# Mixture-of-experts tile loop: transposed rows two tiles ahead, first half's routing moved ahead

## The reference, cut to what matters

```
h      = layernorm(x); h = (h - mean over tokens) / sd over tokens
h      = h * gamma(subject) + beta(subject)              # a small network per batch
probs  = softmax(h @ router_w)                            # 8 experts
gates, idx = top_k(probs, 2); gates = gates / gates.sum(-1)
hid    = relu(h @ exp_w1[e] + exp_b1[e])                  # 128 -> 512, for each expert
eout   = hid @ exp_w2[e] + exp_b2[e]                      # 512 -> 128
out    = x + sum over the two chosen experts of gate * eout
```

## Time and profile before

| | us |
|---|---|
| median of 3 runs | 141.12 |
| lowest and highest | 140.81, 142.25 |
| the profiled execution | 139.6 |
| its span, first to last instruction | 137.8 |
| TensorE busy | 98.7 (72%) |
| DVE busy | 54.7 (40%) |
| ACT busy | 48.7 (35%) |
| GpSimd busy | 47.3 (34%) |

### The profile page before, as it was taken

How to read it: one execution, slowest core, us unless ns; L and a number is a source line. 1 busy time by engine, 2 the same in 40 slices (tenths; PEclk the granted TensorE clock), 3 DMA queues, 4 the chain that set the end, 5 groups by cost and what they waited for, 6 DMA issues and landing times.

```text
span 137.8 us, 2307 instructions
## 1 busy us (share of the span) xinstructions
PE 98.7 (72%) x668; PEld 82.5 (60%) x668; DVE 54.7 (40%) x250; ACT 48.7 (35%) x145; POOL 47.3 (34%) x62
## 2 busy tenths in 40 slices
PE   6999997699999999007866777667777677773000
PEld 2597984498595949006856777567776567763000
DVE  0679988195699160300133222232222332222053
ACT  3615654713806161000543334433344333341000
POOL 7594400006876772000022343223432223434100
PEclk9999999959999999855699999999999999999755
DMA  4999994000110117992041748898988788000183
GB/s 97 351 305 412 412 402 198 2 0 13 44 41 26 40 36 179 415 379 67 0 139 65 233 177 252 270 277 243 237 229 259 230 288 320 8 3 0 52 276 129
DMA packets 12140, 24.47 MB, mean 178 GB/s; under 512 B 1895, under 2 KB 7223, under 8 KB 12128
## 3 DMA queue, kind: packets, MB, share of 16 engines
q1 hardware_dynamic: 9936, 22.01, 48.7%
q0 software_dynamic: 1184, 1.46, 3.2%
q10 hardware_dynamic: 1008, 0.86, 2.1%
HBM read 18.04 MB, written 7.28 MB: 184 GB/s over the span
## 4 chain that ended last, share of the span: by engine, by line
PE 36%; DMA 26%; issue 18%; POOL 8%; DVE 6%; ACT 2%; POOLq 1%; SPq 1%; DVEq 0%; ACTq 0%
PE zt L864 12%; DMA sums_dram<-yg_t,rt 9%; PE zt L874 8%; POOL rows_dram L502 7%; DMA wt<-in_exp_w_dram 7%; DMA rows_dram<-h_row,row_i 4%; DMA rt<-rows_dram 3%; PE zt L686 3%; DMA sums<-sums_dram 2%; PE zt L701 2%; PE zt L828 2%; DVE acc L1244 1%; PE yt L855 1%; PE zt L835 1%; PE aux L746 1%
## 5 line engine op out<-in xcount | busy, mean ns | idle before, releaser
L670 ACT ACTIVATE hid_t<-zt,wt 128x128 f32<-128x128 f32 x84 | 23.9, 368 | 48.5 <-PE zt L864 48.5
L511 POOL DMA_INDIRECT sums_dram<-yg_t,rt x21 | 20.4, 970 | 54.9 <-DVE yg_t L1231 54.6
L864 PE MATMUL zt<-xT_t,wt 128*128 128x128 f32 x168 | 25.6, 299 | 15.9 <-issue 13.4
L864 PEld LDWEIGHTS zt<-xT_t,wt 128*128 128x128 f32 x168 | 22.0, 204 | 19.6 <-issue 15.8
L1231 DVE SCALAR_TENSOR_TENSOR yg_t<-zt,rt,b_t 128x128 f32<-128x128 f32 x21 | 7.4, 351 | 44.6 <-PE zt L874 44.6
L874 PE MATMUL zt<-wt,hid_t 128*128 128x128 f32 x168 | 22.1, 275 | 0.0
L874 PEld LDWEIGHTS zt<-wt,hid_t 128*128 128x128 f32 x168 | 20.5, 193 | 0.0
L502 POOL DMA_INDIRECT rows_dram<-h_row,row_i x16 | 15.8, 988 | 6.0 <-issue 4.3
L621 ACT ACTIVATE hid<-zt,we 128x512 f32<-128x512 f32 x16 | 11.0, 688 | 12.6 <-PE zt L828 11.7
L828 PE MATMUL zt<-h,we 128*128 128x512 f32 x30 | 14.3, 601 | 0.0
L844 PEld LDWEIGHTS yt<-we,hid 128*128 128x128 f32 x64 | 9.0, 227 | 0.5 <-issue 0.5
(11 more groups left out here) (170 smaller groups left out, 116.5 us busy)
## 6 DMA issues: line engine op xcount, KB each, us to landing
wt<-in_exp_w_dram SPq DMA_DIRECT2D x21, 578.0 KB, 5.1
rows_dram<-spare_rows SPq DMA_DIRECT2D x1, 3120.0 KB, 13.1
rt<-rows_dram SPq DMA_DIRECT2D x21, 65.0 KB, 3.5
we<-in_exp_w_dram SPq DMA_DIRECT2D x2, 578.0 KB, 10.3
sums_dram<-zeros SPq DMA_DIRECT2D x2, 512.0 KB, 14.8
f<-in_x_dram SPq DMA_DIRECT2D x2, 256.0 KB, 4.5
ft<-in_x_exchanged_dram SPq DMA_DIRECT2D x2, 256.0 KB, 5.2
sums<-sums_dram SPq DMA_DIRECT2D x4, 128.0 KB, 3.0
```

The source lines that it names most:

```text
L511: pool.indirect_dma_start(sums_dram, bass.IndirectOffsetOnAxis(ap=rt[:, n, ID_AT:ID_AT + 1].bitcast(I32), axis=0), yg_t[:, n, :], None, bo ...
L670: act.activation(hid_t[:, i % 2, c, :], z_t[i % 2][:, c * P:(c + 1) * P], ACT.Relu, bias=bias).then_inc(tile_hid, 1)
L864: last = pe.matmul(z_t[i % 2][:, c * P:(c + 1) * P], wt[:, i % W_SLOTS, c * P:(c + 1) * P], xT_t[:, i % 2, :], start=True, stop=True)
```

## The change

- *Tile loop.* DVE copies the transposed rows of tile i+2, not of tile i+1, before it gates tile i.
- *SP.* The weights of each of the first five tiles are issued as soon as its code is loaded, not after all 21 codes. Twelve codes are loaded before the wait for the row scatters, the others one by one in the alternating loop, behind the row load.
- *Shares.* They are written by DVE into `h_row` directly; GpSimd's copy L495 and its semaphore go.
- *First half's routing.* On TensorE, logits, row transposes and ranks of half 0 move ahead of most of expert 0's layer 1 (which is no longer cut in pairs). On DVE, the choices of half 0 move ahead of the second half's normalising; the shares of half 0 are woven into the second half's inverse deviation (`shares_and_inverse_sd`), and row numbers come before the normalised copies. On ACT the exponential and the row copies of half 0 move ahead.
- *Dense experts.* The order becomes half by half: `turn(e, n)` = 2n + e. Expert 0 and expert 1 on half 0 are computed before expert 0 and 1 on half 1; DVE's gates and additions for half 0 are placed among the second half's front.

The core of the diff (the renamed uses of `share` and of `y_d[e][n]` left out):

```diff
+def turn(e, n):
+    return n * DENSE + e
...
-            codes = [sp.value_load(code[i:i + 1, 0:1], min_val=0, max_val=SPARE) for i in range(TILES)]
+            def next_code():
+                i = len(codes)
+                codes.append(sp.value_load(code[i:i + 1, 0:1], min_val=0, max_val=SPARE))
...
+            sp.wait_ge(code_ready, 1)
             for i in range(W_SLOTS):
+                next_code()
                 tile_weights(i)
+            while len(codes) < CODES_FIRST:
+                next_code()
             sp.wait_ge(rows_out, 16 * B * TOPK)
...
                     tile_rows(i + ROW_SLOTS - W_SLOTS)
+                if len(codes) < TILES:
+                    next_code()
...
-                pool.wait_ge(share_ready, 2 * (n + 1))
-                pool.tensor_copy(h_row[:, :, batches(n), GATE_AT],
-                                 share[:, batches(n), :].rearrange("p b k -> p k b")).then_inc(row_gate_ready, 1)
-                pool.wait_ge(row_gate_ready, n + 1)
+                pool.wait_ge(share_ready, TOPK * (n + 1))
...
-            act.wait_ge(w_in[0], 16)
+            inverse_sd_features(1)
+            gate_exponent(0)
+            token_rows(0)
             hidden(0, 0, 0)
-            inverse_sd_features(1)
-            token_rows(0)
             hidden(0, 0, 1)
             normalise(1)
...
-            layer1_by_pairs()
+            wait_for_h(0)
             logits(0)
+            token_rows(0)
+            layer1(0, 0, 0)
             layer1(0, 0, 1)
+            ranks(0)
             layer1(0, 0, 2)
-            token_rows(0)
+            layer1(0, 0, 3)
+            pe.wait_ge(h_row_ready, TOPK)
+            layer2(0, 0, 0)
             pe.wait_ge(xs_ready, BH)
             norm_transposed(1)
-            layer1(0, 0, 3)
-            ranks(0)
-            pe.wait_ge(h_row_ready, TOPK)
-            layer2(0, 0, 0)
             for c in range(1, C):
                 layer2(0, 0, c)
+            pe.wait_ge(w_in[1], 16)
+            layer1(1, 0, 0)
             wait_for_h(1)
             logits(1)
-            layer1(0, 1, 0)
             token_rows(1)
-            layer1(0, 1, 1)
+            layer1(1, 0, 1)
             ranks(1)
-            layer1(0, 1, 2)
-            layer1(0, 1, 3)
+            layer1(1, 0, 2)
+            layer1(1, 0, 3)
+            pe.wait_ge(acc_done, BH * (turn(0, 0) + 1))
+            for c in range(C):
+                layer2(1, 0, c)
...
             conditioned(0)
             feature_stats(1)
             logit_tops(0)
-            normalise(1)
+            logit_gap(0)
             choices(0)
-            logit_gap(0)
+            shares_and_inverse_sd()
             row_numbers(0)
+            normalised(1)
+            dense_gates(0)
+            add_biases(0, 0)
             moved = token_stats(1)
-            shares(0)
             scale_and_shift(1, moved)
             conditioned(1)
+            add_expert(0, 0)
             logit_tops(1)
+            logit_gap(1)
             choices(1)
-            logit_gap(1)
             row_numbers(1)
             shares(1)
             tile_codes()
-            dense_gates(0)
+            add_biases(1, 0)
+            add_expert(1, 0)
             dense_gates(1)
-            for e in range(DENSE):
-                for n in range(HALVES):
-                    add_biases(e, n)
-                    add_expert(e, n)
+            add_biases(0, 1)
+            add_expert(0, 1)
+            add_biases(1, 1)
+            add_expert(1, 1)
...
             tile_columns(0)
+            tile_columns(1)
             for i in range(TILES):
-                if i + 1 < TILES:
-                    tile_columns(i + 1)
+                if i + 2 < TILES:
+                    tile_columns(i + 2)
                 tile_gated(i)
```

More of the change, by code:

```diff
@@ L42 @@
 PIECES = 4
+CODES_FIRST = 12
 HALF_DIFF2, IDENT = range(2)
@@ L253, in build @@
         z_d = [zt[c % 2][:, half(c // 2)] for c in range(C)]
-        y_d = [[yt[:, half(0)], aux[:, half(1)]], [aux[:, half(0)], yt[:, half(0)]]]
+        y_d = [yt[:, half(0)], yt[:, half(0)], aux[:, half(1)], aux[:, half(0)]]
         xT_ps = [yt[:, HT:HT + P], aux[:, HT:HT + P]]
@@ L401, in _ @@
                              zeros[:]).then_inc(zeroed, 16)
-            sp.wait_ge(code_ready, 1)
-            codes = [sp.value_load(code[i:i + 1, 0:1], min_val=0, max_val=SPARE) for i in range(TILES)]
+            codes = []
+            def next_code():
+                i = len(codes)
+                codes.append(sp.value_load(code[i:i + 1, 0:1], min_val=0, max_val=SPARE))
             def tile_weights(i):
@@ L617, in hidden @@
             def hidden(e, n, c):
-                g = (e * HALVES + n) * C + c
-                act.wait_ge(z_ready, g + 1)
+                act.wait_ge(w_in[e], 16)
+                act.wait_ge(z_ready, turn(e, n) * C + c + 1)
+                if e > 0:
+                    act.wait_ge(y_ready, turn(e, n))
                 act.activation(hid[:, c, half(n)], z_d[c], ACT.Relu,
@@ L646, in _ @@
             hidden(0, 0, 3)
-            gate_exponent(0)
             inverse_sd_tokens(1)
             conditioned(1)
-            hidden(0, 1, 0)
+            hidden(1, 0, 0)
+            gate_exponent(1)
             token_rows(1)
[L652 to L657, removed]
-                for n in range(HALVES):
-                    act.wait_ge(y_ready, (e - 1) * HALVES + n + 1)
-                    for c in range(C):
-                        hidden(e, n, c)
+            for c in range(1, C):
+                hidden(1, 0, c)
+            for e in range(DENSE):
+                for c in range(C):
+                    hidden(e, 1, c)
             for i in range(TILES):
@@ L823, in layer1 @@
             def layer1(e, n, c):
-                g = (e * HALVES + n) * C + c
-                if g >= C:
-                    pe.wait_ge(hid_ready, g - C + 1)
+                if turn(e, n) > 0:
+                    pe.wait_ge(hid_ready, (turn(e, n) - 1) * C + c + 1)
                 pe.matmul(z_d[c], w1(e, c), h[:, half(n)], start=True, stop=True).then_inc(z_ready, 1)
[L830 to L836, removed]
             def layer2(e, n, c):
-                g = (e * HALVES + n) * C + c
-                pe.wait_ge(hid_ready, g + 1)
+                pe.wait_ge(hid_ready, turn(e, n) * C + c + 1)
                 for k in range(BH):
                     tok = slice((n * BH + k) * P, (n * BH + k + 1) * P)
-                    last = pe.matmul(y_d[e][n][:, k * P:(k + 1) * P], hid[:, c, tok], w2(e, c),
+                    last = pe.matmul(y_d[turn(e, n)][:, k * P:(k + 1) * P], hid[:, c, tok], w2(e, c),
                                      start=(c == 0 and k == 0),
@@ L1019, in normalise, with normalised @@
                                        ALU.mult).then_inc(mrs1_ready, 1)
+                normalised(n)
+            def normalised(n):
                 v.wait_ge(rs1_final, n + 1)
@@ new lines, in shares_and_inverse_sd @@
+            def shares_and_inverse_sd():
+                was, now = batches(0), batches(1)
+                v.wait_ge(var1_ready, B)
+                v.wait_ge(rs1_ready, HALVES)
+                squared = mark(v.tensor_tensor(sq1[:, now], rough1[:, now], rough1[:, now], ALU.mult))
+                moved = mark(v.scalar_tensor_tensor(rm1[:, now], mv1[:, now, 0], -1.0, rough1[:, now], ALU.mult, ALU.mult))
+                v.wait_ge(ex_ready, 1)
+                summed = mark(v.tensor_scalar(ex_sum[:, was], ex[:, was], 1.0, None, ALU.add))
+                v.wait_ge(dve, squared)
+                scaled = mark(v.scalar_tensor_tensor(vs1[:, now], mv1[:, now, 1], 1e-5, sq1[:, now], ALU.add, ALU.mult))
+                v.wait_ge(dve, summed)
+                v.reciprocal(share(0, 0), ex_sum[:, was]).then_inc(share_ready, 1)
+                v.wait_ge(dve, scaled)
+                v.scalar_tensor_tensor(rs1[:, now], vs1[:, now], 3.0, rough1[:, now], ALU.subtract,
+                                       ALU.mult).then_inc(rs1_final, 1)
+                v.wait_ge(dve, moved)
+                v.scalar_tensor_tensor(mrs1[:, now], vs1[:, now], 3.0, rm1[:, now], ALU.subtract,
+                                       ALU.mult).then_inc(mrs1_ready, 1)
+                v.wait_ge(share_ready, 1)
+                v.tensor_tensor(share(0, 1), ex[:, was], share(0, 0), ALU.mult).then_inc(share_ready, 1)
@@ L1119, in dense_gates @@
             def dense_gates(n):
                 hb = batches(n)
-                v.wait_ge(share_ready, 2 * (n + 1))
+                v.wait_ge(share_ready, TOPK * (n + 1))
+                both = h_row[:, :, hb, GATE_AT].rearrange("p k b -> p b k")
                 then(v.tensor_tensor(share_if[:, hb],
                                      is_chosen[:, hb, :, 0:DENSE].rearrange("p b k e -> p b e k"),
-                                     share[:, hb, :].unsqueeze(2).broadcast_to((P, BH, DENSE, TOPK)), ALU.mult))
```

(3 more changed lines are left out.)

37 lines of the change are left out of this document (17 added, 20 removed).

## The result

| | before | after |
|---|---|---|
| median of the runs | 140.97 us (140.09 to 142.25, 4 runs) | 123.62 us (121.46 to 125.04, 4 runs) |
| profiled execution, its span | 139.6 us, 137.8 us | 124.08 us, 122.3 us |
| layer 1 of tile 0, 2, 20 starts | 63.2, 69.8, 122.3 us | 53.6, 59.0, 106.5 us |

The ratio is 0.869 [0.853, 0.886]: 17.4 us less by the medians. The forecast was 126.0 (119 to 131).

The account below looks back on a forecast made before the run. Bounds named: row scatters delaying the tiles, then gating ahead of the next copy in each turn. Tile 20 at 107.4 in place of 122.32 saves 14.9 us: 139.6 - 14.9 = 124.7 profiled, scaled by 1.011 to 126.0 us median (119 to 131).

Parts of the forecast that it names:

- First half's routing: Front: half 0's logits at 19.0 us, first row scatter at 25.3 in place of 31.58.
- Codes and weights: SP before the tiles: weights issued 38.2 to 42.9 us, last scatter landed 47.7, first row tile 51.9, 10 us earlier.
- Dense experts: TensorE before the tiles: 32.4 us of work plus 2.1 of waits, ending at 53.5; sets tile 0's start at 55.2.
- Granted in full throughout: Sign of the forecast: TensorE's clock never falls during the run.
- rival 2: Start of the tiles: late rows (2 us) or a clock fall (up to 2.5 us); median 128.6 us, chance 0.12.
- The gap of 0.79: Tile loop: TensorE's 0.79 us standstill each turn, from gating ahead of the next copy on DVE, was to vanish.
- The ring: Tile loop: gating, sums scatter, row load issue, weight load, layer 1; 13.56 us per five tiles, 14.15 with a code load.
- The scatter in the ring: Tile loop: sums scatter lands in 4.3 us (median), seeming to wait for weight loads, despite the page's round-robin rule.
- rival 3: Tile loop: scatters slip past the weights, landing in 2.1 us, ring 11.36; median 119.4 us, chance 0.09.
- Rival 1: Tile loop: ring closes as tightly or copies don't get ahead, turns stay 2.92 us; median 130.4 us, chance 0.14.
- Rival 4: Tile loop: ring is no bound, TensorE sets turns of 2.13 us; median 116.0 us, chance 0.05.
- Rival 5: Tile loop: crowded transfers make it slower, by 1% from a ring of 19.0 us on; chance 0.02.

Follow-up runs that it names:

- e9: Changed kernel with SP's old order: all 21 codes loaded first, then the five weight loads; 130.66 us, ratio 0.937 to the kernel before.
- e4: Changed kernel without three of four chunks of layer 2 of expert 1 on the second half; 122.53 us, ratio 0.882 to the kernel before.
- e6: e3 with the first tile's copy ahead of the last dense expert's additions on DVE; 110.80 us, ratio 0.791 to the kernel before.
- e11: e3 without three of four chunks of layer 2 of expert 1 on the second half; 110.89 us, ratio 0.792 to the kernel before.
- e5: The changed kernel itself again, unaltered, on the chip of e6 to e8; 124.01 us (122.09 to 127.06).
- e2: Changed kernel with the copy one tile ahead again, so the front's part alone; 129.61 us, ratio 0.924 to the kernel before.
- e1: Kernel before with only the copies taken two tiles ahead; 132.56 us, ratio 0.955 to the kernel before.
- e12: e10 with five weight loads issued first and the other three behind the first eight row loads; 108.73 us, ratio 0.779 to the kernel before.
- e3: Changed kernel with 16 row slots in place of 8 and row loads six tiles ahead of the weights; 111.21 us, ratio 0.794 to the kernel before.
- e7: Changed kernel with six weight slots in place of five; 116.71 us, ratio 0.835 to the kernel before.
- e10: e6 with eight weight slots, all eight issued with the first codes; 111.75 us, ratio 0.802 to the kernel before.
- e8: Changed kernel with all 21 codes loaded before the rows, none in the loop; 123.51 us (120.88 to 123.95).

## Why the prediction was right, point by point

*First half's routing.* Forecast: first scatter 25.3, ninth 36.2, last 45.2. Measured: 24.32, 34.90, 43.93. Right, about 1 us on the safe side from the first one on.

*Codes and weights.* The weights were to go out from 38.2 to 42.9; SP's timeline has all five within 37.08 to 42.04. The landing of the last scatter was mis-sized: I took 2.5 us because "most of the weights are over by then". Issued at 43.93, it took 4.7 us and held SP's row loads until 48.83: the scatters amid the weights take 5.0 at the median, those ahead of them 2.4. It cost nothing, since the row loads then landed in 1.9 us and not in the 4.07 taken from the earlier trace rows, so that the rows were there at 50.7, ahead of my 51.9. What I had not seen is how much this step is worth: by e9 the early weights carry some 7 of the front's 9 us, since the row loads would else queue behind them. The other parts of the front (routing, shares, order of the dense experts) were not tried one by one.

*Dense experts.* Their end was forecast at 53.5 and came at 52.1; tile 0 at 55.2 and came at 53.64. The work at full clock was right, 32.5 us where the sum had 32.4 (TensorE was busy for 32.51 of the 33.50 us from 18.57 to 52.07, at a granted clock of 1.00); the waits were mis-sized, 1.0 us and not 2.1, and the start came at 18.57, not 19.0. The mechanism is in the chain above: layer 2, additions, copy, layer 1. It leads the rows by so little that an earlier start alone brought no measurable gain at the end in e4, e6 and e11. The margin between rows and dense end was forecast at 53.5 - 51.9 = 1.6 us; it was 52.1 - 50.7 = 1.4.

*The clock.* "Granted in full throughout" was wrong for the profiled run: rival 2's clock part came. The chain's layer 1 of tile 0 at 53.64 took 1.13 us, that of tile 1 at 55.35 took 1.99, and tile 2 started at 58.95, 1.7 us later than in e5. Rival 2 had priced this at up to 2.5. The half clock of the kernel before was worth 2.0 us, where the estimate was 2.5: from tile 0 to tile 2 it took 6.6 us, and e2, which has the same order in the loop and the clock in full, takes 4.6. Not controlled here: why the clock falls in one run and not in the next.

*Tile loop.* "The gap of 0.79 has no cause left": right, by e1 and e2. The unstalled turn was mis-sized: 1.90 us, not 2.13. I had summed layer 1 at 1.13, its length after a wait. TensorE's timeline in a stretch without waits:

```profile
60.85 1.06 PE L860 MATMUL zt<-xT_t,wt 128*128 128x128 f32 x8
61.74 0.27 PE L851 MATMUL yt<-ident,rt 128*128 128x128 f32 x1
61.85 1.06 PE L870 MATMUL zt<-wt,hid_t 128*128 128x128 f32 x8
62.74 1.06 PE L860 MATMUL zt<-xT_t,wt 128*128 128x128 f32 x8
```

From start to start, layer 1 takes 0.89 there, the transpose 0.11 and layer 2 0.89. 
The ring was forecast at 14.15 us for five tiles with a code load and 13.56 without. Measured from tile 1: 55.35, 69.05, 83.3, 96.3, that is 13.7, 14.3 and 13.0 (tile 16 did not wait for its weights, so the last is no stall of the ring). Its parts in the chain above: 2.30 to the gating (forecast 2.26), 1.18 to the scatter's issue (1.18), 4.80 to its landing at SP (4.3), 0.55 to the weights' issue (0.72), 5.00 until layer 1 starts (5.1). Tile 20 was forecast at 107.4 and came at 106.5.

*The scatter in the ring.* The row scatters show again what the earlier trace rows did: 5.0 us amid weight loads, 2.4 without. The forecast put the page "DMA: Bandwidth & Descriptors" of the Trainium skill (Queues, rings and completion order: round-robin between queue rows, a packet at a time) against this; by that rule, as the forecast read it, the time would have been rival 3's 119.4, and the trace disagrees with that reading once more. Which part of the path makes the scatter wait (the DMA engines, or the completion) was not tried.

*The rivals.* Rival 1, turns that stay at 2.92, is what e2 shows, and the changed kernel doesn't. Rival 4, no ring at all, is not this kernel, but it is e12: the ring can be opened. Rival 5 would have needed landings of 14.9 us together; in the turn above they are 9.6. Denser traffic alone did not bring them near that. In e3 weight loads took 5.0 us at the median and sums scatters 4.2, as in the changed kernel (5.2 and 4.2); in e12, the densest, they did grow, to 6.3 and 5.4, 11.7 together.

*The sum.* 124.7 for the profiled execution, measured 124.08. That it comes so close is luck: the start was 1.6 us earlier than forecast, and the fall of the clock, which the sum had at nothing, took 1.4 of it back by tile 2 (58.95, forecast 59.1). The loop from there took 47.6 us for a forecast of 48.3, and the end 15.8 for 15.5. With the clock in full, as the forecast had it, e5's profiled execution took 122.09: 2.6 us less than the sum. The median was scaled by 1.011 to 126.0 and came at 123.62, below the profiled execution this time, whose mean granted clock (0.936) was under that of the two shorter executions (0.958 and 0.964).

## What to carry to other kernels

When a change removes the wait that sets a loop's turn, write down at once the ring that comes next, with all its latencies, and divide by the slots: here 13.8 us over five weight slots is 2.8 us a turn, only a little under the 2.9 removed, and one slot more (e7) was worth 5.5 us in the profiled runs, 7 by the medians. Slots of two kinds on one in-order queue bind one another: the weights could not run ahead because the row loads in front of them waited for scatters (e3). And on a queue, put the small transfers that a start hangs on ahead of the large ones, or the large ones long before: the same loads in another order were worth some 7 us in e9 and 3 in e12 (against e10).

## What the runs showed of the hardware beyond the forecast

- A DMA share near 0.9 was no limit. The changed kernel's loop shows 0.88 at 269 GB/s between 80.4 and 94.3 us while TensorE waits for weights; with a wider ring the share goes to 1.0 and the rate to 358 GB/s, and TensorE waits for next to nothing.
- Small loads issued directly behind large ones on their own queue took longer: the first eight row loads, 65 KB each, took 1.9 us at the median with no weight load beside them, and 5.0 to 7.1 us behind five weight loads of 578 KB (e9). Whether they wait in the queue or at the DMA engines was not taken apart.
- A stretch at half clock (0.50 or 0.51 granted, the 1.2 GHz level) followed a wait of TensorE of 1.5 to 1.7 us at the start of the tiles in some runs (the changed kernel, e10) and not in others with much the same wait (e5, e8); with a wait of 7 us it began during the wait and lasted 10 us (e9).
